# A graph layer and a routed feed-forward on one core: merges and one-hot builds as two float32r halves, gate logits on TensorE, and the split between gathered and dense nodes moved by one tile

## The reference

```
x = x + segment_sum(layernorm(x)[src] * edge_weight, dst) @ W.T + b
n = layernorm(x)
x = x + shared_mlp(n) + sum over the top 2 of 4 experts of topw * expert_mlp(n)
```

## Time and profile before

| | us |
|---|---|
| median of 3 runs (lowest, highest) | 400.21 (397.77, 401.97) |
| the profiled execution | 397.88 |
| its span | 395.8 |
| busy: PE, DVE, ACT, POOL | 356.3, 279.5, 202.2, 277.5 |

### The profile page before, as it was taken

How to read it: one execution, slowest core, us unless ns; L and a number is a source line. 1 busy time by engine, 2 the same in 40 slices (tenths; PEclk the granted TensorE clock), 3 DMA queues, 4 the chain that set the end, 5 groups by cost and what they waited for, 6 DMA issues and landing times.

```text
span 395.8 us, 8049 instructions
## 1 busy us (share of the span) xinstructions
PE 356.3 (90%) x2319; PEld 284.6 (72%) x2319; DVE 279.5 (71%) x1199; ACT 202.2 (51%) x551; POOL 277.5 (70%) x294
## 2 busy tenths in 40 slices
PE   5996669989869999999999999999978999998773
PEld 3785568767768788877787877787866777766562
DVE  6598999692998999628899677662199522777371
ACT  2566796482487997023959953222085321243330
POOL 7777777777777777777777777777777777776000
PEclk9999879999989999999999999999999999999999
DMA  6999549844444554434343434343433344334000
GB/s 205 375 367 339 149 101 310 223 104 108 102 107 100 122 135 98 110 107 131 102 130 104 129 102 134 104 125 104 134 95 107 106 134 133 105 100 130 14 15 25
DMA packets 53857, 53.69 MB, mean 136 GB/s; under 512 B 32522, under 2 KB 43508, under 8 KB 53684
## 3 DMA queue, kind: packets, MB, share of 16 engines
q0 software_dynamic: 13536, 36.98, 31.3%
q1 hardware_dynamic: 35220, 10.53, 11.5%
q10 hardware_dynamic: 5056, 5.64, 4.1%
HBM read 46.64 MB, written 6.48 MB: 134 GB/s over the span
## 4 chain that ended last, share of the span: by engine, by line
PE 64%; DVE 11%; SPq 10%; issue 6%; DMA 4%; ACT 3%; DVEq 0%; ACTq 0%
PE agg_ps L1220 15%; PE hid_ps L1252 14%; SPq L739 7%; PE window_ps L1153 7%; PE tok_ps L1301 5%; DMA x_sb<-in_x 4%; PE agg_ps L1189 4%; PE build_ps L1207 3%; PE hid_ps L1265 3%; PE tok_ps L1299 3%; PE hid_ps L1261 3%; DVE gate_x L1678 3%; DVE high_node L1620 2%; PE agg_ps L1207 2%; ACT h L1006 1%
## 5 line engine op out<-in xcount | busy, mean ns | idle before, releaser
L832 POOL DMA_INDIRECT rows<-normalised_rows,src_all x246 | 239.8, 975 | 75.0 <-issue 75.0
L1220 PE MATMUL agg_ps<-xn_all,dense 128*128 128x256 f32 x350 | 79.7, 381 | 0.0
L1252 PE MATMUL hid_ps<-xt,pack 128*128 128x256 f32 (+2 forms) x336 | 70.6, 356 | 5.2 <-ACT xt L987 4.9
L1220 PEld LDWEIGHTS agg_ps<-xn_all,dense 128*128 128x128 f32 x350 | 65.3, 190 | 9.6 <-ACT dense L968 0.7
L1252 PEld LDWEIGHTS hid_ps<-xt,pack 128*128 128x128 f32 x336 | 56.0, 190 | 14.8 <-issue 8.0
L918 ACT ACTIVATE low_1h<-iota,lo_f 128x128 f32<-128x128 f32 x182 | 57.5, 393 | 0.6 <-ACT xn_all L904 0.4
L1006 ACT ACTIVATE h<-hid_ps,pack 128x256 f32<-128x256 f32 (+2 forms) x84 | 32.8, 442 | 41.4 <-PE hid_ps L1252 41.3
L1620 DVE TENSOR_SCALAR high_node<-iota,hi_f,own_w 128x125 f32<-128x125 f32 x182 | 50.6, 355 | 1.9 <-PE agg_ps L1207 1.6
L816 POOL DMA_INDIRECT rows<-in_x,src_first x36 | 35.3, 981 | 11.0 <-issue 10.4
L1678 DVE CUSTOM_DVE_ANT_0 gate_x<-xn,shared 128x256 f32<-128x256 f32 x100 | 41.9, 480 | 0.3
L1153 PE MATMUL window_ps<-rows,select 128*32 128x256 f32 x564 | 36.1, 384 | 1.7 <-DVE select L1570 1.7
(11 more groups left out here) (171 smaller groups left out, 525.5 us busy)
## 6 DMA issues: line engine op xcount, KB each, us to landing
rows<-normalised_rows,src_all POOLq DMA_INDIRECT x246
x_sb<-in_x SPq DMA_DIRECT2D x6, 512.0 KB, 10.3
normalised_rows<-xn_all ACTq DMA_DIRECT2D x6, 512.0 KB
records<-in_rec SPq DMA_DIRECT2D x184, 1.5 KB
out<-y SPq DMA_DIRECT2D x10, 256.0 KB
dense<-in_x_cols ACTq DMA_DIRECT2D x4, 512.0 KB, 8.9
pack<-in_packed SPq DMA_DIRECT2D x1, 1540.5 KB, 9.4
x_sb<-in_x SPq DMA_DIRECT2D x3, 256.0 KB, 10.7
```

The lines of the kernel that those rows point to most:

```text
L832: pool.indirect_dma_start(rows[:, b % RING * BATCH + pos, :], None, table[:, :], bass.IndirectOffsetOnAxis(ap=src_all[:, c:c + 1], axis=0) ...
L1220: last = pe.matmul(dense_ps[0:r, t * D:(t + 1) * D], dense[:, h, t * P:t * P + r], xn_all[:, h, :], start=(h == 0 and t == 0), stop=(h == ...
L1252: last = pe.matmul(by_half(u.hid_ps[b % 2])[:, m % 2, 0:tok], w, u.xt[:, k, 0:tok], start=(k == 0), stop=(k == KD - 1))
```

## The change

Five things, in one diff.

1. `windows`, `place`, `low_1h` and `high_node` become float32r. A merge multiplies the placement by two halves of each window: ACT's copy of it, rounded to float32r, and the rest, which DVE subtracts (`window_rest`, and `raw_rest` for the first three batches). A build does the same with the weight in the one-hot (`own_parts`), so its one-hot has two halves of 126 columns, made by one DVE instruction of 252 elements with two tensor operands.
2. The gate logits come from PE: four float32 products a tile (two of k, as two instructions each) of the turned rows with the 256x4 gate weights, between `copy_turned` and `layer1`; DVE adds the gate bias. `gates` goes.
3. The border between gathered and dense nodes moves: 2101 nodes gathered in 267 chunks (23 batches, the last of 3; nine units), 1024 dense (8 tiles, 208 windows). There are 13 units in place of 14.
4. `KEEP`, the number of windows held, goes from 6 to 5. Some buffers share memory: raw windows lie in `h2`, so `relu2` of the first unit waits for `s_raw_turned`; `shared` holds 260 columns in place of 1284.
5. The planner has other durations, ranks and unit order, so that all four lists are new.

```diff
-G_TILES = 17
+G_TILES = 16
 G_NODES = G_TILES * P + HALF
-G_CHUNKS = -(-(G_NODES + MARGIN) // STEP)
+G_CHUNKS = -(-(G_NODES + MARGIN) // (STEP * TRIPLE)) * TRIPLE
-LAST = TRIPLE * 2
+LAST = TRIPLE
-KEEP = 6
+KEEP = 5
+KEYS = HI * WIN + HI * WIN % 2
-UNIT_ORDER = "G0 D0 G1 G2 D1 G3 G4 G5 D2 G6 G7 D3 G8 G9"
+UNIT_ORDER = "G0 D0 G1 G2 D1 G3 D2 G4 G5 G6 G7 D3 G8"
...
-        windows = sb("windows", [P, KEEP, D])
-        place = sb("place", [P, KEEP, PAIR])
+        windows = sb("windows", [P, KEEP, 2, D], F32R)
+        place = sb("place", [P, KEEP, PAIR], F32R)
...
-        low_1h = sb("low_1h", [P, RING, GROUP, P])
+        low_1h = sb("low_1h", [P, RING, GROUP, P], F32R)
+        own_parts = sb("own_parts", [P, N_WINDOWS, 2], F32R)
+        high_node = sb("high_node", [P, RING, GROUP, 2, KEYS], F32R)
...
             def select_batch(b):
                 pe.wait_ge(s_select, b + 1)
-                if b:
+                if b > RAW_BATCHES:
+                    pe.wait_ge(s_rest, b - RAW_BATCHES)
+                elif b:
                     pe.wait_ge(s_windows, b)
...
-                        last = pe.matmul(sums_of(unit)[:, t * D:(t + 1) * D],
-                                         place[0:full, b % KEEP, at:at + P],
-                                         windows[0:full, b % KEEP, :],
-                                         start=(b == batches[0]), stop=(b == batches[-1]))
+                        for half in range(2):
+                            last = pe.matmul(sums_of(unit)[:, t * D:(t + 1) * D],
+                                             place[0:full, b % KEEP, at:at + P],
+                                             windows[0:full, b % KEEP, half, :],
+                                             start=(b == batches[0] and half == 0),
+                                             stop=(b == batches[-1] and half == 1))
...
-                    last = pe.matmul(built_in(k)[:, j * width:(j + 1) * width], low_1h[:, k % RING, j, :],
-                                     high_node[:, k % RING, j, :],
-                                     start=True, stop=True)
+                    for half in range(2):
+                        last = pe.matmul(built_in(k)[:, j * KEYS:(j + 1) * KEYS], low_1h[:, k % RING, j, :],
+                                         high_node[:, k % RING, j, half, :],
+                                         start=(half == 0), stop=(half == 1))
...
+            def gate_products(q):
+                if q == 0:
+                    pe.wait_ge(s_w, 16)
+                pe.wait_ge(s["xt"], q + 1)
+                for t in range(UNITS[q].T):
+                    for k in range(KD):
+                        last = pe.matmul(logit_ps[:, t, :], u.xt[:, k, t * P:(t + 1) * P], gate_w_sb[:, k, :],
+                                         start=(k == 0), stop=(k == KD - 1))
+                last.then_inc(s["gated"], 1)
...
+            def window_rest(b):
+                full = P if batch_size(b) == BATCH else SLOT * len(quad(b, 0))
+                dve.wait_ge(s_windows, b + 1)
+                dve.tensor_tensor(windows[0:full, b % KEEP, 1, :], window_ps[0:full, 0:D],
+                                  windows[0:full, b % KEEP, 0, :].bitcast(F32), ALU.subtract).then_inc(s_rest, 1)
...
-                    last = dve.tensor_scalar(high_node[:, r, j, :], iota[:, 0:HI * WIN],
-                                             hi_f[:, at + j:at + j + 1], own_w[:, at + j:at + j + 1],
-                                             ALU.is_equal, ALU.mult)
+                    last = dve.scalar_tensor_tensor(
+                        out=high_node[:, r, j, :, :], in0=iota[:, 0:KEYS].unsqueeze(1).to_broadcast([P, 2, KEYS]),
+                        scalar=hi_f[:, at + j:at + j + 1],
+                        in1=own_parts[:, at + j, :].bitcast(F32).unsqueeze(2).to_broadcast([P, 2, KEYS]),
+                        op0=ALU.is_equal, op1=ALU.mult)
...
-            def gates(q):
-                done = E * sum(other.T for other in UNITS[:q])
-                dve.wait_ge(s["xn"], q + 1)
-                for t in range(UNITS[q].T):
-                    for e in range(E):
-                        if done >= 2:
-                            dve.wait_ge(s_gate_x, done - 1)
-                        dve.tensor_tensor_reduce(
-                            out=gate_x[:, done % 2, :], in0=u.xn[:, t, :], in1=gate_w_sb[:, e, :], scale=1.0,
-                            scalar=gate_b_sb[:, e:e + 1], op0=ALU.mult, op1=ALU.add,
-                            accum_out=u.logit[:, t, e:e + 1]).then_inc(s_gate_x, 1)
-                        done += 1
```

More of the change, by code:

```diff
@@ L9 @@
 BF16 = mybir.dt.bfloat16
+F32R = mybir.dt.float32r
 I32 = mybir.dt.int32
@@ L221, in placed @@
     def placed(batches):
-        raw = [at("rawout", b) for b in batches if b < RAW_BATCHES]
-        return needs(at("windows", batches[-1]), *raw)
+        return needs(*[at("rawrest" if b < RAW_BATCHES else "rest", b) for b in batches])
     def needs(*times):
@@ L242, in unit_steps @@
             summed = lambda: of("merge")
-            first = [("pe", "merge", sum(0.432 * len(b) for _, b in merges_of(u)),
+            first = [("pe", "merge", sum(0.23 * len(b) for _, b in merges_of(u)),
                       lambda: needs(placed(mine), at("place", mine[-1]),
@@ L249, in unit_steps @@
         return first + [
-            ("dve", "bias", 0.07 + 0.265 * T, lambda: needs(66.0, prior("bias", one))),
+            ("dve", "bias", 0.07 + 0.265 * T, lambda: needs(66.0 if u.kind == "G" else 77.5, prior("bias", one))),
             ("dve", "residual", 0.35 + 0.66 * T,
@@ L293, in fixed @@
                 row = land(b) and land(b) + 2.8
-                offer(needs(at("select", b), row, at("windows", b - 1) if b else 0.0), RANKS["batch"], ("batch", b), 1.43)
+                offer(needs(at("select", b), row, (at("rest", b - 1) if b > RAW_BATCHES else at("windows", b - 1)) if b else 0.0), RANKS["batch"], ("batch", b), 1.43)
             if k < len(GROUPS):
@@ L396, in schedule @@
         if engine == "pe":
-            if begin - free["pe"] > COLD_AFTER:
+            idle.append((begin, begin - free["pe"]))
+            if sum(gap for to, gap in idle[-12:] if to > begin - LATELY) > COLD_AFTER:
                 cold = begin + COLD
+            took *= ISSUE
             took += min(took, max(0.0, cold - begin) / 2)
@@ L661, in build @@
         steps_of_unit = (
-            "x1 stats var std rstd xn turned xt top low ex total inv gate gtop "
-            "ahead tied tied_before glow gex order rank kept ktotal kinv parts mix_turned mixt "
+            "x1 stats var std rstd xn turned xt gated top low ex total inv gate gtop "
+            "ahead tied glow gex rank kept ktotal kinv parts mix_turned mixt "
             "h1a h1b h1 l2 h2 spread mixed end y").split()
@@ L1060, in _ @@
                     relu1(q, 2)
-                    relu2(q)
+                    relu2(q, in_order=False)
         @block.tensor
@@ L1661, in normalise @@
                     dve.wait_ge(s["turned"], q)
-                    dve.wait_ge(s_gate_x, E * sum(other.T for other in UNITS[:q]))
                 for t in range(T):
```

156 lines of the change are left out of this document (92 added, 64 removed).

## The result

The changed kernel takes **409.75 us** (median of 4 runs, 408.21 to 410.76) against 401.09 for the kernel before in the same comparison (397.77 to 404.2): ratio 1.0245, 95% interval 1.0198 to 1.0292. It is slower, by 2.0 to 2.9%. The forecast was 387.5, its range 379 to 398; of the rivals, C had named 410. Times are medians of all runs; where some runs of a kernel or of its neighbour fell in a slower state of the chip, the ratio leaves them out.

A forecast was written before the change was run, and what follows sets the result against it. POOL's gathers and PE's work were taken as nearly level bounds, with PE the bound after the change. 7.3 us less PE work plus 5 less idling take 12.3 off the span: 387.5 us, range 379 to 398.

The forecast's parts named there:

- rival C: 128-column weight loads bound PE's small build and gate products: PE's sum +15.0 us, time 410, slower; chance 0.10.
- The builds: PE's window builds: 416 float32r records at 0.065 us, 27.0 in place of 40.5, so -13.5; other end +5.7.
- The merges: PE's merges: 88 float32r records at 0.11 us, 9.7 in place of 19.9, so -10.2; other end -0.9.
- the gates: Gate products moved to PE: 100 records at 0.08 us, +8, between +6 and +11.
- PE's sum: All changes in PE's work: selections, merges, builds, dense products, gates and fixed costs add up to -7.3 us.
- The gathers: POOL's gather stream: 15 fewer at 1.28 us, so the last starts 19.2 us earlier, at 344.1.
- A gap in the gathers: Sign against the forecast: POOL waits for free rows, so PE's order paces the gathers and the 19 us shrink.
- DVE's sum: DVE's work: gates -43, one-hots +30.4 and smaller terms sum to +5, so it stays near 284 us.
- the idling: PE's waiting: 3 us more from 45 to 85, 5 less later, 3 less in the tail; net -5 us.
- Rival D: DVE's one-hot builds bound at 0.43 us each, PE idles 4 us more: time 397, no change told; chance 0.17.
- Rival E: Float32r isn't faster, each half costs a whole product: builds and merges together +70, time above 460; chance 0.02.
- The chain behind the last gather: Work after the last gather, one unit with 181 nodes: unchanged, costed at nothing, so POOL alone allows span 376.6.

The follow-up runs named there:

- e6: Changed kernel with build operands in bfloat16 and the 252-column one-hot by one-tensor `tensor_scalar`, weight split left out: 392.81 us, ratio 0.9828 to the kernel before.
- e1: Changed kernel with build operands `low_1h` and `high_node` in bfloat16 instead of float32r, same records and DVE instructions: 408.46 us, ratio 1.022 to the kernel before.
- e3: Changed kernel with each merge as one float32 product instead of two float32r halves, the rest still made but unused: 416.48 us, ratio 1.041 to the kernel before.
- e5: Changed kernel with the 252-column one-hot by `tensor_scalar` (one tensor) instead of two tensors, weight split left out: 403.05 us, ratio 1.0074 to the kernel before.
- e7: Changed kernel with float32 one-product builds and gates back on DVE, lists planned anew under the changed kernel's ranks: 419.98 us, ratio 1.051 to the kernel before.

## Why the prediction was wrong

**The builds were mis-sized.** The step "The bfloat16 transposes of 128 columns stand 0.31 - 0.25 = 0.06 apart; the other end is today's 0.111. I take 0.065, by the row nearest in passes" failed. Three successive entries in PE's timeline after give the start-to-start distance:

```profile
193.12 1.19 PE L1228 MATMUL build_ps<-high_node,low_1h 128*128 128x126 f32 x8
194.16 1.05 PE L1228 MATMUL agg_ps<-high_node,low_1h 128*128 128x126 f32 x8
195.05 1.08 PE L1292 MATMUL hid_ps<-h,pack 128*128 128x256 f32 x4
```

(195.05 - 194.16)/8 = 0.111 a record, and 1.04/8 = 0.130 for the group behind other work: 416 records are 46 to 54 us, not 27. The float32 transposes of the earlier trace rows, which also load 128 columns for each record, stood 0.11 apart, and that was the right neighbour. The same 126 columns in bfloat16 take 0.057 (e6), so the type decides, not the count of columns. The weight loads (PEld) differ with it: the first row is of the changed kernel, the second of e1 (durations ns min/median/max, first and last start).

```profile
L1228 PEld LDWEIGHTS agg_ps<-high_node,low_1h x160: 186/192/192, 109.5 to 299.5; 128*128 128x128 f32 x160
L1228 PEld LDWEIGHTS agg_ps<-high_node,low_1h x160: 95/98/100, 109.3 to 296.3; 128*128 128x128 bf16 x160
```

The load's type and the stream's type were always changed together, so that it is the load is argued, from these rows and from the gate products below: they stream 4 columns behind the same load and cost 0.10. The Trainium skill ("TensorE: Matmul & The Clock Gate", LDWEIGHTS (loading the stationary operand), with Weight-path perf modes) gives columns over 1.2 GHz, 0.107 for 128, and a fast load for other types than FP32. The rows agree, if float32r counts as FP32 there: the forecast had quoted this rule, under rival C, and given that rival 0.10.

**The merges were right.** Two halves of 256 columns:

```profile
183.44 1.44 PE agg_ps L1209 x12
184.88 0.79 PE mid_ps L1263 x8
187.50 0.84 PE agg_ps L1228 x8
```

In the chain of waits (columns as the earlier trace rows) the first is 0.12 a record, forecast 0.11 against 0.216 before; 88 of them are 10.6 us, and in e3 float32 merges cost 7 us more. Here a stream of 256 columns gains from float32r, and one of 126 behind the same load doesn't. The second line is the gates: 0.79/8 = 0.10, near the dear end of the bounds 0.06 and 0.11; the forecast took 0.08, so 2 us more.

**PE's sum.** With 0.111 and 0.10 it is -1.8 - 9.3 + 5.7 + 10.8 + 10 - 0.6 = +14.8, rival C's sum, and the page says +20.3. Of the other 5 us, 4.0 are gone in e5, whose edit touches no instruction of PE (372.6). Busy time is stretched where the clock is low (24 selections take 2.79 us at 48.37 and 1.50 at 190.05), and from 45 to 85 the clock is 0.79 there and 0.73 here; how much of the 4.0 that makes, and the rest, no run splits. Small slips in the forecast's arithmetic (50 x 0.2178 is 10.9, and its margins give 387.9 where it says 387.5) change nothing.

**The gathers were not 19.2 us earlier.** The step "15 fewer, at 1.28 us: the last starts 19.2 us earlier, at 344.1" failed, and nothing in the forecast prices a DVE instruction by what it does to POOL. "A gap in the gathers" stood among what would make it wrong, but with free rows as the cause. Here are three long gathers, in POOL's timeline, and what DVE did, in its own:

```profile
78.70 5.26 POOL L845 DMA_INDIRECT rows<-normalised_rows,src_all  x1 [0.30 <-issue]
...
155.06 4.32 POOL L845 DMA_INDIRECT rows<-normalised_rows,src_all  x1 [0.30 <-issue]
...
215.17 3.22 POOL L845 DMA_INDIRECT rows<-normalised_rows,src_all  x1 [0.30 <-issue]
```
```profile
76.32 6.35 DVE L1670 SCALAR_TENSOR_TENSOR high_node<-iota,hi_i,own_parts 128x252 fp32r<-128x252 f32 x16
...
154.87 3.21 DVE L1670 SCALAR_TENSOR_TENSOR high_node<-iota,hi_i,own_parts 128x252 fp32r<-128x252 f32 x8
...
212.79 4.79 DVE L1670 SCALAR_TENSOR_TENSOR high_node<-iota,hi_i,own_parts 128x252 fp32r<-128x252 f32 x12
```

Each began inside a run of one-hots and ended 0.8 to 1.3 us after the run did (83.96 and 82.67, 159.38 and 158.08, 218.39 and 217.58), which is about one gather's own 0.95; behind the third, another four one-hots had begun at 217.69. They are 10.0 of the 23.0 us; the rest are small extensions of many gathers, and e5 keeps 5.6 of them. Not every gather in such a run is held: the one at 77.33, inside the run from 76.32, took 1.07, and those inside the runs of eight at 95.28 and 123.75 no more than 1.27. That the form is a cause is shown by e5, which alters only it. The Trainium skill ("SBUF — State Buffer", Who interferes with whom) says that a DVE instruction with two SBUF inputs contends with a GpSimd instruction that reads SBUF, by an exclusive lock that it describes as held for one instruction; the gathers read `src_all`, so the direction agrees. But one instruction is 0.40 here and the longest hold was 5.26 - 0.95 = 4.3 us, some eleven of them. The same section tells of a `tensor_tensor` with two SBUF inputs that didn't stall a DMA, and infers that the issue of a DMA wants the pair's write side, which such an instruction leaves alone. The gate products of the next sentences fit that; by it the one-hots shouldn't have held a gather. Nor do two inputs suffice: in the kernel before, the gate products (two tensors of 256) run eight in a row from 342.10, and the gathers at 342.96 and 344.21 took 0.95 each. What sets those apart wasn't tried; each has an accumulator read behind it, the one-hots have nothing between them. The second tensor of the one-hots is also one column spread over 252.

**DVE's sum was right, and the idling in total.** One-hots stand 6.35/16 = 0.40 apart (forecast 0.38), DVE is at 284.0, and PE idles 7.1 us less (forecast 5). From 85 to the last merge it idles 5.2 us less, as forecast (5), but the other two terms were off and cancelled in part: idling from 45 to 85 was to grow by 3 and fell by 0.7, and in the tail it was to fall by 3 and fell by 1.1. So the total is right in part by luck. Rival D had no part in it. Rival E is out (a merge half is 0.12). Rival C's mechanism holds and its time, 410, is met, but partly by chance: by e1, with cheap builds alone the time stays at 408.

**The chain behind the last gather was put at nothing.** "Behind it comes the same chain of one unit with 181 nodes ... I cost that at nothing. So POOL alone would allow a span of 376.6" failed too. 32.5 us stood behind the last gather before, 46.8 after, and 390.9 - 345.0 = 45.9 in e6, where the gathers and the builds are as forecast. PE is busy 36.4 us of these 45.9 (in 345 to 390.9), and was 21.7 of the 32.5 before: the list has a whole unit, D3, ahead of the last one there, where it had the half unit G8. So with this list gathers that end at 345 give some 391, and e6 is there. No other list was tried on e6.

**What is still open.** e6 has the forecast's premises and is at 392.8, not 387.5: PE's work is right within 1 us, but it idles 40.9 us and not 34.5. So the credit for idling held in the changed kernel, where PE had 26.6 us more to do, and not in e6. Its clock is at 0.64 from 45 to 65; how much of it that makes wasn't tried apart. Nor is it settled how far e7 is the list's doing.

## What to carry to other kernels

Price a cheaper type by what the instruction is limited by: where 128 columns are loaded for each 126 that stream, ask for a row with the same load, and give the rule that speaks against the change the weight of the row that bears it out. When an instruction's form changes on DVE, look at every queue that POOL issues, not only at DVE's own time. Where two bounds are level, undoing one cause shows little, so run the pair (1.3 and 6.7 us alone, 16.9 together). And when the list of an engine changes, count anew what it has to do behind the last event of the other bound (32.5 us before, 46 here).

## What the runs showed of the hardware that was not expected

- Long runs of `scalar_tensor_tensor` with two SBUF tensors (252 float32 elements, 0.40 apart) stretched single indirect gathers from 0.95 to up to 5.26 us, 18 us in the kernel, though not every gather within them; the same length by `tensor_scalar` (0.326 apart, 5.21 us without a break) held none.
- A float32r record of 126 columns behind a load of 128 costs 0.111 to 0.130, as much as a float32 one (0.111) or more; with 256 columns it costs 0.12 where a float32 one costs 0.216, and float32 needs as many records for one product as two float32r halves; bfloat16 with 126 is at 0.057.
- A float32 record that streams 4 columns behind a load of 128 costs 0.10 to 0.11.
